# Cross attention with two softmax stages on one core: the last two tiles' parts interleaved, the last tile's division moved to the output stage, evacuations moved ahead of the sums' copies, the context first in setup

## The reference

```
query = x @ Wq ; keyt = enc @ Wk ; valt = enc @ Wv
hs = mha(query, keyt, valt)                       # softmax over 124 keys
ca_q1 = einsum('btc,th->bch', ca, Wq_ca)          # 384 rows of 640
ca_q1 = ca_q1[:, linspace(0, 383, 2048), :]       # 2048 rows, repeated
ca_hs1 = mha(ca_q1, x, x)                         # softmax over 2048 keys
ca_hs2 = mha(ca_hs1 @ Wq, ca @ Wk_ca, ca @ Wv_ca) # softmax over 4 keys
out = (hs + ca_hs2) @ Wout + b_out + x
```

## Time and profile before

| what | value |
|---|---|
| median of 3 runs | 782.83 us (780.24, 784.38, 782.83) |
| profiled execution | 779.47 us |
| its span | 777.7 us |
| mean granted clock of TensorE over the span | 0.991 of full speed |
| PE, DVE, ACT, POOL busy | 97%, 69%, 48%, 22% of the span |

### The profile page before, as it was taken

The page is one execution under the profiler, slowest core; times in us unless marked ns, Lnnn a source line. Parts: engine busy times, 40 slices in busy tenths (PEclk is TensorE's granted clock), DMA queues, the critical chain, the costliest instruction groups (busy, mean ns, idle before and its releaser), DMA issues.

```text
span 777.7 us, 13016 instructions
## 1 busy us (share of the span) xinstructions
PE 754.7 (97%) x4969; PEld 706.1 (91%) x4969; DVE 538.2 (69%) x910; ACT 375.7 (48%) x938; POOL 171.8 (22%) x232
## 2 busy tenths in 40 slices
PE   7999999999899999999999999999899999999998
PEld 5979999999688879999999999999878888999997
DVE  3456887888899985345546887888799995544442
ACT  1634445445588963223234445445479892222220
POOL 7025832111200001432220522111110001112130
PEclk9999999999899999999999999999989999999999
DMA  9424433443210025644434333444220002354431
GB/s 294 121 91 132 93 89 89 99 107 104 75 52 1 1 71 157 219 149 159 158 91 85 89 90 89 99 107 104 89 82 1 1 1 99 122 184 156 149 116 64
DMA packets 112821, 79.32 MB, mean 102 GB/s; under 512 B 91756, under 2 KB 93292, under 8 KB 112760
## 3 DMA queue, kind: packets, MB, share of 16 engines
q1 hardware_dynamic: 112760, 78.50, 34.4%
HBM read 48.56 MB, written 29.88 MB: 101 GB/s over the span
## 4 chain that ended last, share of the span: by engine, by line
PE 92%; DVE 4%; issue 2%; ACT 1%; DMA 0%; SPq 0%; DVEq 0%
PE PS L1138 30%; PE PS L1335 18%; PE PS L1321 8%; PE PS L1206 6%; PE PS L1112 6%; PE PS L1237 6%; PE PS L1228 5%; PE PS L1270 4%; PE PS L1084 2%; PE PS L1044 2%; PE PS L1303 1%; DVE e_hi L916 1%; PE PS L1254 1%; PE PS L1095 1%; PE PS L1159 1%
## 5 line engine op out<-in xcount | busy, mean ns | idle before, releaser
L1138 PE MATMUL PS<-mm_hi,xT_hi 128*128 128x280 f32 (+3 forms) x480 | 159.3, 332 | 0.0
L829 DVE TENSOR_REDUCE mpart<-PS 128x4 f32<-128x512 f32 x192 | 131.9, 687 | 39.5 <-PE PS L1112 39.2
L1138 PE MATMUL PS<-mm_lo,xT_hi 128*128 128x280 f32 (+3 forms) x480 | 157.5, 328 | 0.0
L1138 PE MATMUL PS<-mm_hi,xT_lo 128*128 128x280 f32 (+3 forms) x480 | 157.4, 328 | 0.0
L502 POOL TENSOR_TENSOR ex<-ex,rinv 128x992 f32<-128x992 f32 x32 | 59.1, 1846 | 223.2 <-DVE rinv L823 223.2
L613 ACT ACTIVATE ex<-PS,neg 128x124 f32<-128x124 f32 x256 | 90.0, 364 | 7.3 <-DVE gs L811 7.2
L1138 PEld LDWEIGHTS PS<-mm_hi,xT_hi 128*128 128x128 f32 x480 | 90.5, 189 | 0.8 <-issue 0.5
L1138 PEld LDWEIGHTS PS<-mm_hi,xT_lo 128*128 128x128 f32 x480 | 90.4, 188 | 0.4
L1138 PEld LDWEIGHTS PS<-mm_lo,xT_hi 128*128 128x128 f32 x480 | 90.3, 188 | 0.2
L924 DVE TENSOR_TENSOR e_lo<-e,e_hi 128x1536 fp32r<-128x1536 f32 (+1 forms) x46 | 77.3, 1688 | 4.8 <-ACT e_hi L664 4.0
L1112 PE MATMUL PS<-gT,aTm 128*128 128x256 f32 x384 | 76.6, 281 | 0.7 <-DVE mpart L829 0.7
(11 more groups left out here) (146 smaller groups left out, 1452.4 us busy)
## 6 DMA issues: line engine op xcount, KB each, us to landing
ex_kept<-ex SPq DMA_DIRECT2D x32, 512.0 KB, 2.9
ex<-ex_kept SPq DMA_DIRECT2D x32, 512.0 KB, 3.9
xin<-in_x SPq DMA_DIRECT2D x128, 80.0 KB, 2.9
xin<-in_x SPq DMA_DIRECT2D x32, 320.0 KB, 3.2
out<-res SPq DMA_DIRECT2D x32, 320.0 KB, 2.3
raw_kept<-raw SPq DMA_DIRECT2D x5, 512.0 KB, 2.6
mm_lo<-raw_kept SPq DMA_DIRECT2D x10, 186.0 KB, 3.9
wq_in<-in_L_xattn_Wq SPq DMA_DIRECT2D x2, 800.0 KB, 9.1
```

Source lines behind the costliest of these rows:

```text
L829: nc.vector.tensor_reduce(mpart[:, n // 2, :, 2 * (n % 2):2 * (n % 2) + 2, i].rearrange("p s k -> p k s"), PS[:, 6 + N % 2, :].rearrange(" ...
L1138: last = mul(PS[:, slot(T, k), p0:p0 + w], l[:, i % 2, j, :], rr[:, m0:m0 + w], start=(j == 0 and n == 0), stop=(n == 2), skip_group_check ...
```

## The change

It has four parts.

1. *Interleaving.* The last two tiles of a batch (14 and 15) give their parts in the order (14, 0), (14, 1), (15, 0), (14, 2), (15, 1), (15, 2). A new table `PARTS` holds this order; the banks and the semaphore counts follow from a part's place in it (`part(T, k)`). PE's loop body becomes `scores(...)`, called by `step(i)` for tiles 0 to 13 and by `last_steps()` for the last six parts, with the units placed over these 90 matmuls; ACT and DVE get the orders that belong to it. Two related edits: the minimum of the last part moves behind `as_` on DVE, and of the four narrow copies of `aTs` ACT now makes r = 2, 3 and DVE r = 0, 1.
2. *Last tile's division.* `normalise(b, 15)` leaves the score stage. SP stores tile 15 as soon as its exponentials are done, and POOL divides it after it has been loaded again, in `gathered(15)`.
3. *Evacuations first.* At the beginning of the output stage ACT evacuates `pT(1)` before `take(1)`, DVE does `pT(0)`, `take(1)`, `pT(1)` and then `heads_sum(0)`, and PE puts `nT(0)` behind the seventh matmul of the own heads.
4. *Context first.* SP issues the context's transfer first, then a third of Wk, then `wqca`, then the other thirds. PE transposes the context first, into three banks that DVE copies one by one; the key matmuls go over the thirds of Wk, with the transposes of `wqca` and the first key transposes (into bank 2) behind the first third.

The diff, cut to its core:

```diff
+def part_order():
+    last = [(TILES - 2, 0), (TILES - 2, 1), (TILES - 1, 0), (TILES - 2, 2), (TILES - 1, 1), (TILES - 1, 2)]
+    return [(i, k) for i in range(TILES - 2) for k in range(3)] + last
...
+        def part(T, k):
+            return T // TILES * 3 * TILES + PART_AT[T % TILES, k]
         def slot(T, k):
-            return (3 * T + k) % 4
+            return part(T, k) % 4
...
-            sp.dma_start(wqca_in[:, :], wqca).then_inc(wqca_in_s, 16)
             sp.dma_start(ctx_tok[:, :, :], ctx_in.rearrange("b t n -> t b n")).then_inc(ctx_in_s, 16)
-            sp.dma_start(wk_in[:, 0], wk.rearrange("(c p) n -> p c n", p=P)).then_inc(wk_in_s, 16)
+            for c in range(CT):
+                sp.dma_start(wk_in[:, 0, c, :], wk[c * P:(c + 1) * P, :]).then_inc(wk_in_s[c], 16)
+                if c == 0:
+                    sp.dma_start(wqca_in[:, :], wqca).then_inc(wqca_in_s, 16)
...
-                sp.wait_ge(norm_made, (b + 1) * TILES)
+                sp.wait_ge(exp_made, 3 * (b + 1) * TILES)
                 sp.dma_start(ex_kept[b, TILES - 1], ...)
...
-                for i in range(3, TILES):
+                for i in range(3, TILES - 1):
                     normalise(b, i)
...
                 def gathered(i):
                     pool.wait_ge(ex_in[i % 2], (b * GROUPS + i // 2 + 1) * 16)
+                    if i + 1 == TILES:
+                        normalise(b, i)
+                        pool.wait_ge(norm_made, (b + 1) * TILES)
...
# ACT, end of the score stage
-                        if i + 1 == TILES and h == 5:
+                        if i + 1 == TILES and h == 4:
                             first_rows()
-                    for r in (0, 2):
+                    for r in (2, 3):
...
+                g(TILES - 1)
+                exps(TILES - 1, 0)
+                exps(TILES - 2, 2)
+                exps(TILES - 1, 1)
                 exps(TILES - 1, 2)
...
                 pT(0)
+                pT(1)
                 take(1)
-                pT(1)
...
# DVE, the last two tiles
+                least(i, 0)
+                g(i)
+                unit(i - 1, 3)
+                y_low(i - 1, 1)
+                unit(i - 1, 4)
+                unit(i - 1, 5)
+                least(i - 1, 2)
+                unit(i, 0)
+                unit(i, 1)
+                y_low(i - 1, 2)
+                unit(i, 2)
+                inv(i - 1)
+                unit(i, 3)
+                least(i, 1)
+                dve.wait_ge(mx_made, b * UNITS_B + i * UNITS)
+                nc.vector.tensor_reduce(m14[:, :], ...)
+                unit(i, 4)
+                unit(i, 5)
...
                 y_low(TILES - 1, 1)
+                least(TILES - 1, 2)
...
-                for r in (1, 3):
+                for r in (0, 1):
...
# DVE, output stage
-                take(1)
                 pT(0)
+                take(1)
+                pT(1)
                 heads_sum(0)
                 soft2(0)
                 probs2(0)
-                pT(1)
...
# PE
-                LAST_AT = {3: (-1, 3), 8: (-1, 4), 13: (-1, 5), 26: (0, 0), 29: (0, 1), 33: (0, 2), 36: (0, 3), 40: (0, 4), 43: (0, 5)}
+                LAST_AT = {3: (-2, 3), 12: (-2, 4), 21: (-2, 5), 33: (-1, 0), 37: (-1, 1), 41: (-1, 2), 45: (-1, 3), 49: (-1, 4), 53: (-1, 5),
+                           58: (0, 0), 62: (0, 1), 66: (0, 2), 70: (0, 3), 74: (0, 4), 78: (0, 5)}
...
+                def last_steps():
+                    units_at = {q: (TILES - 1 + d, n) for q, (d, n) in LAST_AT.items()}
+                    for n, (i, k) in enumerate(PARTS[-6:]):
+                        scores(i, k, 15 * n, units_at, {26: TILES - 2, 52: TILES - 1})
...
-                pe.wait_ge(nsa_made, SETS * (b + 1))
-                pe.wait_ge(nsd_made, SETS * (b + 1))
-                nT(0)
...
                         for j in range(KT):
+                            if n == 0 and j == 3:
+                                pe.wait_ge(nsa_made, SETS * (b + 1))
+                                pe.wait_ge(nsd_made, SETS * (b + 1))
+                                nT(0)
```

More of the change, by code:

```diff
@@ L855, in _ @@
                 nc.vector.memset(ybuf[:, :, :, :].rearrange("p i (m t) d -> p i m t d", t=3)[:, :, :, 1:3, YW].bitcast(F32), 1.0).then_inc(ones_made, 1)
-                for i in range(1, TILES):
+                for i in range(1, TILES - 1):
                     least(i - 1, 2)
@@ L1028, in _ @@
             mul = nc.tensor.matmul
-            pe.wait_ge(wqca_in_s, 16)
             pe.wait_ge(ident_made, 1)
-            for j in range(KT):
-                last = nc.tensor.transpose(PS[:, 0, j * NT:(j + 1) * NT], wqca_in[:, j * P:(j + 1) * P], ident[0:NT, 0:NT])
-            last.then_inc(wca_ps, 1)
             pe.wait_ge(ctx_in_s, 16)
@@ new lines, in scores @@
+                def scores(i, k, at, units_at, stacks):
+                    T = b * TILES + i
+                    t = part(T, k)
+                    if t >= 4:
+                        b0, (i0, k0) = (t - 4) // (3 * TILES), PARTS[(t - 4) % (3 * TILES)]
+                        if k0 == 0:
+                            pe.wait_ge(exp_made, t - 3)
+                        else:
+                            pe.wait_ge(yl_made, 2 * (b0 * TILES + i0) + k0)
+                    if k == 0:
+                        pe.wait_ge(xTl_made, T + 1)
+                    if b and i == 0 and k != 1:
+                        pe.wait_ge(res_made, b * TILES - (1, 0, 0)[k])
+                    for j in range(KT):
+                        m0, w = mm_at(j, k)
+                        p0 = ps_at(j, k)
+                        for n, (l, rr) in enumerate(((xT_hi, mm_hi), (xT_lo, mm_hi), (xT_hi, mm_lo))):
+                            last = mul(PS[:, slot(T, k), p0:p0 + w], l[:, i % 2, j, :], rr[:, m0:m0 + w],
+                                       start=(j == 0 and n == 0), stop=(n == 2), skip_group_check=True)
+                            if at in stacks:
+                                g_stack(stacks[at])
+                            if at in units_at:
+                                unit(*units_at[at])
+                            at += 1
+                    last.then_inc(sc_ps, 1)
@@ L1173, in _ @@
                 pe.wait_ge(mmy_made, (b + 1) * (1 + 2 * len(YRUNS)))
-                for i in range(TILES):
+                for i in range(TILES - 2):
                     step(i)
+                last_steps()
                 pe.wait_ge(gT_made, (b + 1) * TILES)
```

131 lines of the change are left out of this document (49 added, 82 removed).

## The result

| | kernel before | kernel after |
|---|---|---|
| median (runs) | 781.54 us (4) | 770.76 us (4) |
| lowest and highest | 777.74, 784.38 | 769.91, 771.25 |
| profiled execution | 779.47 us | 771.25 us |
| its span, mean granted clock | 777.7 us, 0.991 | 769.5 us, 1.000 |

The changed kernel is 1.4% faster: the ratio of the times is 0.9864, with a 95% interval of 0.9818 to 0.991. The direction was right, the size was not: 10.8 us between the medians instead of 6.2.

A forecast was written before the change was run, and what follows sets the result against it. PE, working 97% of the 777.7 us span, was taken to bound the kernel. Terms: 5.4 (end of scores) - 0.2 (output head) + 1.0 (setup) = 6.2 us, off the median 782.83: 776.6, stated as 776.5, range 771.0 to 781.0.

The forecast's parts named there:

- Line 1180 and the chain behind it: End of scores: the `as_` transposes start some 0.4 us behind the last score matmul instead of 1.98; first `e_lo` follows earlier.
- The first `e_hi`: End of scores: DVE's first `e_hi` copy takes 0.95 us instead of 3.09 once POOL's division is moved away.
- The tail's price: End of scores: 2.7 us gained per batch, 5.4 in all (bounds 3.8 and 6.8), with a shorter clock fall still expected.
- Setup: Setup, once: the context's transfer first gains 1.0 us (0.35 to 1.9).
- the sum's own branch for a change at 8.0: Setup: if PE's pace changed at 8.0, the query weights' transposes would start at 17.7 instead of 19.65.
- The head: Head of the output stage: evacuations first cost 0.2 us in all (bounds -0.5 and +2.4), a wait for `p2` replacing another.
- The division's: Output stage: tile 15's division behind its reload costs 0; without cover up to 1.9 us per batch.
- The base and the clock: Whole kernel: the gain was put on the median of three runs, 782.83 us, 3.4 above the profiled execution.
- Rival (a): End of scores stays at half clock and setup gains only its head start: 3.7 us gain, 779; chance 0.13.
- (b): Head of the output stage gains as it looks, 1.2 us more per batch: 8.8 us gain, 774; chance 0.07.
- (c): Output stage: the new 1.4 us wait for `p2` lets the clock fall; slower, 786; chance 0.05.
- (d): Last two tiles: DVE is late, PE waits there, line 1180's wait only moves; 3.2 of 5.4 lost, 779.7; chance 0.09.

The follow-up runs named there:

- e1: The kernel before, run once more with no edit: 780.36 us, ratio 0.9989.
- e4: The kernel before with only the last tile's division moved to the output stage: 778.2 us, ratio 0.9961.
- e11: The kernel before with the interleaved last tiles and the moved division, without the new setup and output-stage head: 774.42 us, ratio 0.9917.
- e9: The changed kernel, run once more with no edit: 770.23 us, ratio 0.987 to the kernel before.
- e3: The kernel before with only the evacuations put ahead of the sums' copies at the head of the output stage: 780.93 us, ratio 0.9999.
- e5: The kernel before with only the last two tiles interleaved, the division left where it was: 780.2 us, ratio 0.9982.
- e7: The changed kernel with the sums' copies put back ahead of the evacuations: 771.59 us, ratio 0.9875 to the kernel before.
- e8: The changed kernel with the third pass of the own heads ahead of the products that read `p2`: 771.39 us, ratio 0.9873 to the kernel before.
- e12: The changed kernel with the products that read `p2` moved behind five of the third pass's twelve matmuls: 770.98 us, ratio 0.9878 to the kernel before.
- e6: The changed kernel with three repeats of DVE's maximum added so PE waits before the `as_` transposes again: 781.62 us, ratio 0.9994 to the kernel before.
- e2: The kernel before with only the new setup, the context's transfer first: 780.39 us, ratio 0.9984.
- e10: The kernel of e8, run once more: 771.32 us, ratio 0.9878 to the kernel before.

## Why the prediction was wrong in size

The landmarks of the batches (us behind T), by kernel:

| kernel, batch | fall behind T | e_lo | p2 |
|---|---|---|---|
| before, both | 6.8 us | 10.96 | 88.07 |
| before (e1), second | none | 10.11 | 87.22 |
| division (e4), both | none | 8.58 | 86.63 |
| both edits (e11), second | none | 7.22 | 84.52 |
| all parts, both | none | 7.22 | 84.46 |
| all parts (e9), first | 6.8 us | 8.05 | 86.05 |

**Line 1180 and the chain behind it** were right, a little cautious: the wait is 0 instead of 0.4, and the `e_lo` pass comes at T + 7.22 instead of T + 7.6. The second `sT` at T + 3.63 instead of T + 4.2 is the same 0.4 and a little more. (The 15th unit stood ahead of the last score matmul before, not of the last but one; nothing hangs on it.) **The first `e_hi`** is 0.96, as said, and e4 shows by itself that the division was what held DVE. The row that made me count it, 3.09, was only one face of it. In one batch each of e1 and e3 the copy came first and took 0.96, POOL's division took 2.54 instead of 1.84, and then the two `e_lo` took 4.95 together instead of 3.43 (e5). The Trainium skill (SBUF — State Buffer, Who interferes with whom) says that the order of issue, not the kind of operation, decides who is blocked; these rows agree.

**The tail's price** is where the first step failed. I wrote: "so I expect the fall again, later and shorter, and take 2.7 per batch". The fall was absent in both batches of the profiled execution, and T to "out" gave 3.62 and 3.65 us. Without a fall on either side T to `p2` gives 87.22 - 84.46 = 2.76 per batch (2.70 without the new head, e11). That this is nearly my 2.7 is luck. I had 3.4 from a batch with a fall (T + 10.96) to one without, and took it down for a fall that did not come. The runs show 3.6 for that comparison: 2.76 of work that starts earlier, and 0.86 for the fall that the kernel before had. The premise that PE runs without a gap from the first `e_lo` pass on cost little here, 2.89 at the pass and 2.76 at `p2`, but it is wrong in e4, where 1.53 became 0.59.

**Setup** was mis-sized: 1.0 forecast. The query weights' transposes started at 19.27 to 20.57 in the six traces with the old setup, 19.88 on average, and at 17.23 to 18.83 in eight traces with the new one, 18.01 on average: 1.9 us. The pace of the weight loads changed at 10.56 to 12.76 in the six, 11.5 on average, and at 7.15 to 10.14 in the eight, 8.4 on average. It did not stay at 11.0 as the sum assumed; the sum's own branch for a change at 8.0 gave 17.7. The first key matmul's weights came only 1.7 us earlier on average, so what moved the change of pace by 3.1 is not shown. The Trainium skill (TensorE: Matmul & The Clock Gate, What's actually happening) says that how many matmuls run slow at a kernel's start varies from run to run; the traces agree, with a scatter of 2.2 us with the old setup and 3.0 with the new one in the time at which the pace changes.

**The head** gained 0.1 per batch (e7, e11) where I had -0.1: the wait for `p2` did take the place of the wait removed, as the sum of 3.03 us from the reciprocal said. **The division's** new place cost nothing (e4).

**The base and the clock** are the rest. The seven of 87 later runs of the kernel before with a clock of 1.000 took 777.76 to 779.89, mean 778.56. The seven of nine runs of the changed kernel that had it took 769.44 to 771.25, mean 770.31. At full clock the change is worth 8.25 us (7.5 to 9.0, from their scatter). The steps explain 2 x 2.78 + 1.9 = 7.5 of it, where 2.78 is T to "out", 93.26 in e1's batch without a fall less 90.48, with the head's 0.1 in it; 7.5 lies at the edge of the interval, and 0.75 has no place of its own. But only one run in twelve of the kernel before keeps its clock, and its median lay at 780.06 to 781.3 beside the experiments, at 780.9 beside e1 to e4, 2.3 us above that mean. The changed kernel keeps it in seven runs of nine (in e9 three of five, where the kernel before beside it has two of eleven) and loses 0.1 in its median. So the step from 776.5 to about 770.4 is made up as follows: 1.9 for the base, since 782.83 was a median of three that lay high; 1.3 for the terms above; 2.2 for falls that no longer happen; 0.7 without a place. I put the gain on top of a median and did not ask how much of that median was lost clock. That was the second failure, and at 1.9 + 2.2 us it is the larger.

**Rival (a)**, half clock behind T, decides only a run now and then (e9). **(b)** is out: e8 and e12 show that the head can give 1.5 or 0.65 per batch only if other work goes into the wait. **(c)**, the fall behind the new wait, was seen in one batch of e3 and in both of e6, and never in the changed kernel's two profiles. **(d)** is out: PE does not wait once in the last two tiles of either batch, and T itself moved by no more than setup explains.

**What stays open** is why the falls come where they come. With 1.3 us of wait per batch restored (e6), all 12 runs had them, but PE's wait alone does not decide: e4 and the second batch of e1 keep the wait of 1.98 us and have no fall behind T. Two of the four parts alone gain 1.6 (e2) and 2.8 us (e5) in their timelines and 0.5 and 0.2 us in their medians, and a third, the division (e4), gains 1.2 in its timeline and 2.7 in its median. The kernel of e8 and e10 does less waiting than the changed kernel and kept clock 1.000 in none of 11 runs, against seven of nine. I had two explanations, chance wherever work is thin, and the adjoining of thin products. The 11 runs speak against pure chance; e12 decides nothing on the second, since its profile has no fall at the head and four of its six runs lost clock at places that are not known. Neither is shown.

## What to carry to other kernels

Before you add up a gain, split the time before into work at full clock and time lost to falls of the clock, run by run; then forecast both separately. A change that removes idle time of PE can gain more than its length (e6, the other way round: 2.6 us of wait put back, 11 us longer), and parts that are worth something in a timeline can be worth next to nothing in the median by themselves (e2, e5), so judge each part by landmarks in the trace as well as by the time. A wait in the profile can hide a blocked engine on its other side: take the blocker away (here POOL's division) before shortening the chain that it blocks, and look for the engine that is late next (ACT and DVE in e4).

## What the runs showed of the hardware

- The granted clock can fall while PE is busy without a pause: 0.52 from 644 to 646 in e10, with PE busy 2.00 of 2.00 us in that window and the one ahead of it. It can also stay at 1.00 through a window in which PE is busy for 0.34 of 1.00 us (204 to 205, after).
- The mean clock does not order the times of one kernel: beside e1 to e4 the runs of the kernel before at 0.991 took 779.0 to 780.0, those at 0.996 took 780.5 to 782.5. A low stretch of 6.8 us behind the last scores lies beside waits for DVE and costs 0.86 us in the kernel before, 1.6 in e9; one of 3.4 us at the head of the output stage, where PE waits for nothing, cost 1.5 in e3 and 1.0 in e8.
- In setup the weight loads stand 0.41 us apart, twice the later 0.21, while the granted clock of the records reads 1.00 (6 to 9 in the kernel after), so the spacing of the weight loads tells more there than the clock column.
- Of VectorE's copy of 128 x 1536 and GpSimd's division, the one that starts second is held up: the copy took 0.96 us and the division 2.54 where the copy started first (e1), 2.57 and 1.85 where the division did (e5).
